# Slot tiles of 128 in pairs with two experts, gelu written back into PSUM, a regrouped tail and spread scatters in a macaron block

## What is computed

```python
def ffn(x):                       # 8 experts, top 2, inner width 512
    weights = softmax(x @ gate_w.T + expert_bias)
    top_w, top_i = top_k(weights, 2); top_w /= sum(top_w) + 1e-6
    out = sum over e of w[e] * (gelu(x @ w_up[e].T) @ w_down[e].T)   # w[e] is 0 for an expert not chosen
    return layernorm(out) + x
x = x + 0.5 * ffn(layernorm(x))
x = x + attention(layernorm(x))
x = x + 0.5 * ffn(layernorm(x))
```

## Time and profile before

| | |
|---|---|
| time before, median of 3 runs | 1254.38 us (1247.94 to 1255.65) |
| the profiled execution's own time | 1255.69 us |
| its span | 1253.9 us |
| mean granted TensorE clock | 0.919 |
| busy: PE, DVE, ACT, POOL | 917.1 (73%), 985.5 (79%), 711.1 (57%), 790.1 (63%) us |
| first FFN, attention, second FFN, tail | to 277, to 1047, to 1204, to 1253.9 us of the span |

### The profile page before, as it was taken

One profiled execution on the slowest core, in us unless ns is written; L12 is line 12 of the kernel. 1 busy time (PEld: TensorE's weight loads), 2 busy tenths in 40 slices (PEclk: granted clock), 3 DMA queues, 4 the chain that ended last, 5 costly groups with the idle time before them and its releaser, 6 DMA issues.

```text
span 1253.9 us, 32419 instructions
## 1 busy us (share of the span) xinstructions
PE 917.1 (73%) x12594; PEld 745.9 (59%) x12594; DVE 985.5 (79%) x2130; ACT 711.1 (57%) x1033; POOL 790.1 (63%) x671
## 2 busy tenths in 40 slices
PE   3303989778977897887888887696887786779900
PEld 2302979666755675665666665575665575679900
DVE  7887787887769899889899888887688975857722
ACT  2112767557754675665666685474665564657712
POOL 2188735817865676776765664498884675577754
PEclk9999999999997998998998998898898887889955
DMA  9332424329990000000000000000000001223251
GB/s 337 131 109 73 141 84 118 92 76 185 196 188 9 8 9 8 6 9 8 6 8 2 2 2 2 1 15 22 23 15 2 6 17 49 62 80 96 78 165 59
DMA packets 99074, 78.26 MB, mean 62 GB/s; under 512 B 8080, under 2 KB 89360, under 8 KB 98672
## 3 DMA queue, kind: packets, MB, share of 16 engines
q1 hardware_dynamic: 89568, 58.18, 19.8%
q0 software_dynamic: 8640, 17.78, 4.6%
q10 hardware_dynamic: 720, 0.23, 0.1%
HBM read 30.07 MB, written 46.09 MB: 61 GB/s over the span
## 4 chain that ended last, share of the span: by engine, by line
DVE 26%; POOL 25%; PE 23%; issue 14%; ACT 7%; DMA 3%; DVEq 0%; POOLq 0%; SPq 0%; ACTq 0%
POOL arena_a L1824 5%; DVE arena_b L1716 5%; POOL xs L782 4%; POOL xs L814 3%; DVE arena_a L1674 3%; PE bank L1477 3%; POOL arena_a L1806 3%; ACT arena_c L1589 3%; DVE arena_c L1712 2%; POOL arena_b L843 2%; PE bank L1401 2%; POOL arena_c L1828 2%; DVE xn_new L477 2%; PE bank L1403 2%; PE bank L1402 2%
## 5 line engine op out<-in xcount | busy, mean ns | idle before, releaser
L1824 POOL TENSOR_TENSOR arena_a<-arena_a 128x1024 f16<-128x1024 f32 x64 | 139.1, 2173 | 70.3 <-ACT arena_a L1589 69.8
L1589 ACT ACTIVATE arena_c<-arena_a 128x1024 f16<-128x1024 f32 x64 | 67.6, 1057 | 176.4 <-DVE arena_a L1674 176.4
L1806 POOL TENSOR_TENSOR arena_a<-arena_b,trig_rows 128x512 f32<-128x512 f32 x128 | 160.0, 1270 | 6.8 <-issue 6.8
L1699 DVE TENSOR_TENSOR arena_b<-bank,decay 128x512 f32<-128x512 f32 x128 | 82.5, 686 | 53.4 <-PE bank L1477 52.8
L1589 ACT ACTIVATE arena_b<-arena_b 128x512 f16<-128x512 f32 x128 | 78.3, 629 | 66.1 <-DVE arena_b L1699 66.1
L1401 PE MATMUL bank<-wo_hi,arena_c 128*128 128x128 f16 x256 | 53.8, 240 | 75.2 <-DVE arena_c L1683 75.2
L1321 POOL DMA_INDIRECT ys<-arena_b,row_at x78 | 84.8, 1087 | 36.3 <-issue 22.6
L814 POOL DMA_INDIRECT xs<-xhl,slot_idx x64 | 78.5, 1227 | 40.4 <-issue 40.4
L995 ACT ACTIVATE arena_c<-bank,s_pre 128x1024 f32<-128x1024 f32 x46 | 51.2, 1113 | 92.2 <-PE bank L930 86.5
L1827 POOL TENSOR_TENSOR arena_c<-arena_c 128x130 f16<-128x130 f32 x64 | 30.6, 479 | 114.6 <-ACT arena_c L1639 114.5
L1716 DVE TENSOR_TENSOR arena_b<-arena_b 128x1024 f16<-128x1024 f32 x64 | 101.2, 1581 | 0.0
(11 more groups left out here) (320 smaller groups left out, 4275.4 us busy)
## 6 DMA issues: line engine op xcount, KB each, us to landing
xs<-blank SPq DMA_DIRECT2D x8, 2210.0 KB, 32.4
xs<-arena_c SPq DMA_DIRECT2D x2, 3072.0 KB, 18.5
arena_b<-xs SPq DMA_DIRECT2D x46, 128.0 KB
ys<-arena_b SPq DMA_DIRECT2D x46, 128.0 KB, 1.8
arena_b<-xs SPq DMA_DIRECT2D x39, 130.0 KB, 2.3
arena_a<-in_w_up SPq DMA_DIRECT2D x1, 2048.0 KB, 12.6
arena_b<-in_w_down SPq DMA_DIRECT2D x1, 2048.0 KB, 13.6
arena_a<-ys SPq DMA_DIRECT2D x8, 256.0 KB, 4.4
```

What stands on the lines that cost most here:

```text
L1589: nc.scalar.activation(dst, src, ACT.Copy, scale=scale).then_inc(done, 1)
L1699: i = nc.vector.tensor_tensor(probs[:, h * BLK:(h + 1) * BLK].rearrange("p (c i) -> p c i", c=TPB), ps_so[:, h, :].rearrange("p (c i) -> p ...
L1806: i = nc.gpsimd.tensor_tensor(q_trig[h], q_relu[h], trig_rows[:, bass.ds(u * BLK, BLK)], ALU.mult)
L1824: nc.gpsimd.tensor_tensor(q_lo, arena_a[:, 0:2 * BLK], q_hi, ALU.subtract).then_inc(a["q_lo_done"], 1)
```

## The change

- A slot tile is 128 slots with an expert of its own, a pair two such tiles. Experts' slots are rounded up to 128. First FFN: 20 pairs a half; second: 36 pairs, `FULL` = 40 tiles (20 pairs). The expert words are 5 in place of 3.
- `up` and `down` loop over the tile s first and the chunk c inside; `up` has 24 matmuls of 128 columns in place of 12 of 256, and a weight address is formed for each (s, c).
- `h32` is the PSUM bank itself: gelu writes over its input, the high and the low part read PSUM. `up` waits for `lo_done` of the pair before last in place of `gelu_done`; ScalarE's wait for `lo_done` is gone.
- Second FFN: a pair is loaded by two DMAs, each with its own row. y is scattered so that a block's two choices lie together, and the tail loads a block by one DMA of 512 KB.
- Tail: buffers for all blocks, blocks in five groups (`TAIL`), the power for a group at a time, the group before added behind it; no wait for `last_z`.
- Attention: the gating of group 0's tokens moves from (5,0..3) to (4,6), (4,7), (5,0) in fewer, larger pieces, its route from (5,4) to (5,1); group 1's gating from (6,6)..(7,1) to (6,6), (6,7), (7,0), its route from (7,2) to (7,1). The scatters of group 0 stand in (5,2) to (6,7) (14 steps, 2 of them with two tiles) in place of (5,5) to (6,7) (11 steps, 5 with two), those of group 1 in (7,2) to (7,7) in place of (7,3) to (7,7).

```diff
-SLOTS, NPAIR, NTABLE = 24 * 2 * P, 23, 24
+SLOTS, NPAIR, NTABLE = 40 * P, 20, 40
-FULL = -(-(2 * P * 24 - E * (2 * P - 1)) // (2 * P))
-SECOND = NTOK * TOPK // (2 * P) + E - 1
+FULL = 2 * (-(-(2 * P * 24 - E * (P - 1)) // P) // 2)
+SECOND = -(-(NTOK * TOPK // P + E - 1) // 2)
+NPACK = NTABLE // 8
...
-        h32 = [take(PAIR * BLK) for _ in range(2)]
...
+        h32 = [ps[:, :, :].rearrange("p c t -> p (c t)") for ps in ps_pre]
...
+        TAIL = ((0, 1), (1, 3), (3, 5), (5, 7), (7, 8))
...
-            nc.vector.tensor_scalar(rt_int[:], rt_incl[:, :, HALF - 1], float(2 * P - 1), None, ALU.add)
+            nc.vector.tensor_scalar(rt_int[:], rt_incl[:, :, HALF - 1], float(P - 1), None, ALU.add)
...
             def expert_at(packs, p):
-                at = ((packs[p // 8] >> (3 * (p % 8))) & 7) * I
-                return nc.s_assert_within(at, 0, (E - 1) * I, skip_runtime_bounds_check_because="three bits")
+                ats = [((packs[t // 8] >> (3 * (t % 8))) & 7) * I for t in (2 * p, 2 * p + 1)]
+                return [nc.s_assert_within(at, 0, (E - 1) * I, skip_runtime_bounds_check_because="three bits") for at in ats]
...
-            def up(G, at_e):
+            def up(G, at):
                 pe.wait_ge(f["x_copied"], G + 1)
                 if G > 1:
-                    pe.wait_ge(f["gelu_done"], G - 1)
+                    pe.wait_ge(f["lo_done"], G - 1)
                 x_hi, x_lo = xs_T[G % 2][:, 0:2 * P], xs_T[G % 2][:, 2 * P:4 * P]
-                for c in range(CH):
-                    w_hi, w_lo = (w[:, bass.ds(at_e + c * P, P)] for w in (wup_hi, wup_lo))
-                    dst = ps_pre[G % 2][:, c // 2, (c % 2) * 2 * P:(c % 2 + 1) * 2 * P]
-                    nc.tensor.matmul(dst, w_hi, x_hi, start=True, stop=False)
-                    nc.tensor.matmul(dst, w_hi, x_lo, start=False, stop=False)
-                    i = nc.tensor.matmul(dst, w_lo, x_hi, start=False, stop=True)
+                for s in range(2):
+                    x = tuple(part[:, s * P:(s + 1) * P] for part in (x_hi, x_lo))
+                    for c in range(CH):
+                        w_hi, w_lo = (w[:, bass.ds(at[s] + c * P, P)] for w in (wup_hi, wup_lo))
+                        cols = (c % 2) * 2 * P + s * P
+                        dst = ps_pre[G % 2][:, c // 2, cols:cols + P]
+                        nc.tensor.matmul(dst, w_hi, x[0], start=True, stop=False)
+                        nc.tensor.matmul(dst, w_hi, x[1], start=False, stop=False)
+                        i = nc.tensor.matmul(dst, w_lo, x[0], start=False, stop=True)
...
-                for c in range(CH):
-                    w_hi, w_lo = (w[:, bass.ds(at_e + c * D, D)] for w in (flat_dn_hi, flat_dn_lo))
-                    for s in range(2):
+                for s in range(2):
+                    for c in range(CH):
+                        w_hi, w_lo = (w[:, bass.ds(at[s] + c * D, D)] for w in (flat_dn_hi, flat_dn_lo))
...
-                        if G > 1:
-                            act.wait_ge(f["lo_done"], G - 1)
-                        nc.scalar.activation(h32[G % 2], ps_pre[G % 2][:, :, :].rearrange("p c t -> p (c t)"), ACT.Gelu,
+                        nc.scalar.activation(h32[G % 2], h32[G % 2], ACT.Gelu,
...
+            both_choices(0)
+            for group, (b0, b1) in enumerate(TAIL):
+                for b in range(b0, b1):
+                    if b + 1 < NBLK:
+                        both_choices(b + 1)
+                    v.wait_ge(last_sum, b + 1)
+                    for t in range(TPB):
+                        i = nc.vector.bn_stats(first_st6[:, b * TPB + t, :], yl[b][:, t, 0, :])
+                    i.then_inc(last_st, 1)
+                    v.wait_ge(last_st, b + 1)
+                    for t in range(b * TPB, (b + 1) * TPB):
+                        i = nc.vector.bn_aggr(first_mv[:, t, :], first_st6[:, t, :])
+                    i.then_inc(last_ag, 1)
...
-            for b in range(NBLK):
-                power(b)
-                if b:
-                    add(b - 1)
-            add(NBLK - 1)
+            for group in range(len(TAIL)):
+                power(group)
+                if group:
+                    add(group - 1)
+            add(len(TAIL) - 1)
...
-                row = sp.value_load(tile_row[0:1, part, t:t + 1], min_val=0, max_val=NROWS - 2 * P)
...
+                for s in range(2):
+                    t = (2 * p + s) % FULL
+                    row = sp.value_load(tile_row[0:1, int(part), t:t + 1], min_val=0, max_val=NROWS - 2 * P)
+                    sp.dma_start(xs_in2[p % NXS][:, s, :], d["xs2"][bass.ds(row, P), :]).then_inc(in_xs2[p % NXS], 16)
...
-                if n == 5 and hp < 4:
-                    for j in ((0,), (1, 2, 3), (4, 5, 6), (7, 8, 9))[hp]:
-                        gating(v, 2, j)
...
+                for i, first in ((2, 4), (3, 6)):
+                    at = NHP * (n - first) + hp - 6
+                    if 0 <= at < 3:
+                        for j in ((0,), (1, 2, 3, 4), (5, 6, 7, 8, 9))[at]:
+                            gating(v, i, j)
+                    if at == 3:
+                        route_next(v, i - 2)
...
-                        at = NHP * (n - 5) + hp - 5
-                        if 0 <= at < 11:
-                            scatter_next(g, 0, ((0,), (1,), (2,), (3, 4), (5, 6), (7, 8), (9, 10), (11, 12), (13,), (14,),
-                                                (15,))[at])
+                        at = NHP * (n - 5) + hp - 2
+                        if 0 <= at < 14:
+                            scatter_next(g, 0, ((0,), (1, 2), (3,), (4,), (5, 6), (7,), (8,), (9,), (10,), (11,), (12,), (13,),
+                                                (14,), (15,))[at])
```

More of the change, by code:

```diff
@@ L742, in route_next @@
                 then(nc.vector.tensor_tensor(rt_pad[:], rt_end[:], rt_full[:], ALU.subtract))
-                then(nc.vector.tensor_scalar(rt_pad[:], rt_pad[:], -1.0, float(2 * P * FULL), ALU.mult, ALU.add))
+                then(nc.vector.tensor_scalar(rt_pad[:], rt_pad[:], -1.0, float(P * FULL), ALU.mult, ALU.add))
                 then(nc.vector.scalar_tensor_tensor(rt_used[:], rt_pad[:], 0.0, rt_full[:], ALU.max, ALU.min))
@@ L956, in ffn_pe @@
                 pe.wait_ge(route_done, i + 1)
-                packs = [pe.value_load(tile_e[0:1, i % 2, g:g + 1], min_val=0, max_val=2 ** 24 - 1) for g in range(3)]
+                packs = [pe.value_load(tile_e[0:1, i % 2, g:g + 1], min_val=0, max_val=2 ** 24 - 1) for g in range(NPACK)]
                 if not was:
@@ L1204, in load_packs @@
                 pe.wait_ge(tiles_done, part + 1)
-                packs.append([pe.value_load(tile_e2[0:1, part, g:g + 1], min_val=0, max_val=2 ** 24 - 1) for g in range(3)])
+                packs.append([pe.value_load(tile_e2[0:1, part, g:g + 1], min_val=0, max_val=2 ** 24 - 1) for g in range(NPACK)])
             load_packs(0)
@@ L1210, in second_pe @@
             for p in range(SECOND + 2):
-                if p == FULL:
+                if 2 * p == FULL:
                     load_packs(1)
@@ L1323, in scatter_y, with power, add @@
                         y_sb2[p % NYS][:, s, :], None).then_inc(out_y2[p % NYS], 16)
-            def power(b):
-                g.wait_ge(last_var, b + 1)
-                nc.gpsimd.tensor_tensor(frstdh[:], fvar4[:], minus_half[:, 0:TPB], ALU.pow).then_inc(last_pow, 1)
-                g.wait_ge(last_pow, b + 1)
-                nc.gpsimd.tensor_tensor(shift4[:], frstdh[:], neg_mean[:], ALU.mult).then_inc(last_line, 1)
-            def add(b):
-                g.wait_ge(last_z, b + 1)
-                x = x_tok[:, b * TPB:(b + 1) * TPB, :]
-                nc.gpsimd.tensor_tensor(x, x, yl[b][:, 0, :, :], ALU.add).then_inc(last_x, 1)
+            def power(group):
+                b0, b1 = TAIL[group]
+                tiles = slice(b0 * TPB, b1 * TPB)
+                g.wait_ge(last_var, group + 1)
+                nc.gpsimd.tensor_tensor(first_rstdh[:, tiles], first_var4[:, tiles], minus_half[:, tiles], ALU.pow
+                                        ).then_inc(last_pow, 1)
+                g.wait_ge(last_pow, group + 1)
+                nc.gpsimd.tensor_tensor(last_shift[:, tiles], first_rstdh[:, tiles], neg_mean[:, tiles], ALU.mult
+                                        ).then_inc(last_line, 1)
+            def add(group):
+                for b in range(*TAIL[group]):
+                    g.wait_ge(last_z, b + 1)
+                    x = x_tok[:, b * TPB:(b + 1) * TPB, :]
+                    nc.gpsimd.tensor_tensor(x, x, yl[b][:, :, 0, :], ALU.add).then_inc(last_x, 1)
             ln_power(g, 1, NBLK - 1)
@@ L1353, in load @@
             def load(p):
-                part, t = (0, p) if p < FULL else (1, p - FULL)
-                if t == 0:
+                part = 2 * p >= FULL
+                if 2 * p in (0, FULL):
                     sp.wait_ge(tiles_done, part + 1)
-                    if part == 0:
+                    if not part:
```

(6 more changed lines are left out.)

122 lines of the change are left out of this document (54 added, 68 removed).

## The result

The changed kernel takes 1301.99 us (median of 4 runs, 1301.11 to 1303.57) against 1254.53 for the kernel before (median of 4): ratio 1.0393, 95% interval 1.0363 to 1.0422. It is slower, as forecast (1280, range 1238 to 1310), and by nearly twice as much. The profiled execution took 1301.11 us, span 1299.2, granted clock 0.935.

What follows compares the result with a forecast made beforehand. TensorE sets the FFNs' pace, its sequencer just short of being the bound; added register operations make it the bound. On 1255.69 us, +21.3 - 5 + 17.2 - 8.3 = +25.2 gives 1280, range 1238 to 1310.

Steps and rivals of the forecast that it cites:

- The pace: Both FFNs: TensorE's sequencer, slowed by register operations, needs 4.35 us a pair in place of 2.87; bounds 3.9 to 4.7.
- the extraction: Register operations on TensorE's sequencer that get a pair's experts from the words: 4 by 0.097, 0.39 us a pair.
- First FFN: 40 pairs for 46, 38 steps by 4.35 us: the last normalisation starts at 298.3 in place of 276.97, +21.3.
- Second FFN: 36 pairs for 39, 28 steps by 4.35 us: the last scatter ends at 1221.1 against 1203.9, +17.2.
- The five loads: Expert words loaded on TensorE's sequencer, 0.65 us each with the delay behind: 3.3 us in each FFN.
- gelu in PSUM: `low` takes 1.2 us (1.15 to 1.36), scatters keep to 0.96; up's wait for lo_done costs 0.
- Attention: Spreading scatters saves part of what steps with two tiles might cost: -5 us, bounds -16 and +8.
- tail: Last scatter to last add: 32.1 us in place of 40.7, taken as -8.3, bounds -6 and -11.
- B: Rival: the sequencer runs ahead cheaply and matmuls set the pace, 2.92 us a pair, 1207 us; chance 0.17.
- C: Rival: only register operations count, matmuls between them are free, 3.9 us a pair, 1251 us; chance 0.14.
- D: Rival: the granted clock falls to 1.2 GHz through both FFNs, 5.6 us a pair, 1362 us; chance 0.03.
- TensorE busy under 75%: Sign named for the forecast being right: TensorE's busy share in both FFNs at steps of some 4.35 us.

Runs made afterwards that it cites:

- run 1: Changed kernel with the weights of both FFNs taken from fixed experts, so no address is computed in registers (words still loaded): 1201.74 us.
- run 2: Changed kernel with only up's low weights from a fixed place, 8 of a pair's 36 register operations fewer, every matmul kept: 1239.66 us.
- run 4: Kernel before, with down's second tile taking its address from a second register holding the same expert, 27 address operations a pair for 18: 1274.39 us, ratio 1.0177.
- run 9: Kernel before with gelu into PSUM, the spread scatters and the new tail together, but tiles of 256 with one expert: 1219.43 us, ratio 0.9736.
- run 5: Changed kernel with gelu's result in SBUF again, up waiting for gelu_done and ScalarE for lo_done: 1297.77 us.
- run 6: Kernel before with gelu written back into PSUM and up waiting for lo_done, nothing else: 1237.31 us, ratio 0.9868.

## Why the prediction was right or wrong

*The mechanism was right.* The sequencer's register operations set the pace of both FFNs (runs 1, 2 and 4). The three other parts gain on the kernel before, and the tiles lose more than these gain. In the ledger: to the 1219.4 of run 9, tiles of 128 with no operations at all would bring -17.7 (run 1, 1201.7, which leaves out the choice of the expert), and the operations +100.

*The pace was mis-sized: 4.66 for 4.35.* This is the term that was off: 1.90 for up, 0.39 for the extraction, 1.75 for down, 0.32 for waits and turn. On the sequencer, as the mean of the eleven whole pairs in the steady stretch from 1187.30, up with the extraction takes 2.39 (forecast 2.29), down 1.91 (1.75), waits and turn 0.36 (0.32). The median steps are those of rows 3, 0.237 for a group of up and 0.113 for an operation of down. But single groups take up to 0.41 and single steps up to 0.28, which lifts the means to 0.254 and 0.119; I had counted every one at the undisturbed price. What holds those few back is not shown. (In the pair shown above down takes 1.84 and waits and turn 0.51; the latter is rare.) Over 38 and 28 steps the 0.31 makes 20 us, as much as the whole miss; what else was off nearly cancels, and that is luck. 4.66 lay inside the bounds of 3.9 to 4.7, at an end.

*First FFN, +36.4 for +21.3.* 11.8 of the 15 are the pace. 2.6 are the start: the third pair's up at 123.55 where I kept 120.97, since I had costed the wait for lo_done at 0. Its loop is indeed covered in the steady run, but at the filling there is no pair before to cover it (1.9 of it is undone in run 5). *Second FFN, +30.0 for +17.2.* 8.7 are the pace; 3.5 are the eight first pairs, up(8) 39.8 behind up(0) where I had 36.3. The five loads took what I had (3.2 above a step at pair 20), and the end behind the last y too.

*gelu in PSUM.* `low` takes 1.27 where I took 1.2, inside my bounds; it is no shorter than from SBUF. That the scatters keep to 0.96 beside it was right, and on tiles of 256 it gains 10.9 in the second FFN. In the changed kernel it gains nothing and may lose up to 4 (run 5): there 12 of 72 scatters are stretched with gelu in SBUF, but at a step of 4.66 GpSimd has time for them, and they end 4.3 us behind the last y in place of 3.4.

*Attention, tail.* -5 stood against -9.2, of which 4.5 are the change's. The size was right by luck, as far as the traces tell: I took it as a share of what the double scatters might cost, and what the traces show is one long conversion less, which I had counted as a risk only. -8.3 stood against -10.5. From VectorE's last operation to the end of the last add are 7.9 us where I had 9.4: GpSimd's queue holds up less than the 5 I added.

*The rivals.* B's condition, a price below 0.074 a slot, is not met, but its number was nearly right for a kernel without the operations: 1207 against 1201.7. C is out: its 0.097 holds for operations next to each other only, and with matmuls between, most steps are 0.112 to 0.124. The Trainium skill ("Advanced Engine Details and Errata", section Sequencer Loop) says that the sequencer executes control instructions itself; runs 1, 2 and 4, where the pair's time follows their number, agree. Run 1 measured 2.90 a pair. By the Trainium skill ("TensorE: Matmul & The Clock Gate", section Back-to-back issue gap), with about 81 ns for a weight load and matmul of 128 columns, it would have been an estimated 4.1; the measurement decides. D is out: the granted clock is 1.00 in all three steady windows shown, and the mean rose from 0.919 to 0.935.

*The check that I named wrongly.* "TensorE busy under 75%" as the sign of a waiting TensorE: it shows 96%.

## What to carry to other kernels

Count an engine's register operations, waits and loads per tile as a resource of their own. Where weights were chosen by an index here, each distinct address cost some 0.11 to 0.12 us on TensorE's sequencer once that set the pace, so the tile must be large enough to pay for its addresses. A change of several parts should be timed part by part: here three good ones hid under a bad one. TensorE's busy share of 96% hid that its own sequencer held it; compare the steps between starts with those in a stretch known to be dense.

## What the runs showed of the hardware that was not expected

Matmuls of 128 columns, each with a weight load of its own, step by 0.056 us at full granted clock for hundreds of instructions (run 1); per column that is within some 2% of those of 256 in the earlier trace rows. `low`, an operation of VectorE, leaves GpSimd's indirect DMAs at 0.96 us when it reads one PSUM and one SBUF tile, while on two SBUF tiles of the same size it stretched a third of them, most to 1.3 (25 of 78 before, 1 of 78 in run 6). Which one starts first matters: before, 29 scatters of y start while a `low` runs, and 25 of these are stretched; 27 others are running when a `low` starts, and none of these is. In run 6 none of the 30 that start during a `low` is.
